# Value products of five halves in eight on high and low parts, placed behind the projection's heads, in a cross-attention and gated feed-forward kernel

## The reference

```python
x  = layer_norm(features);  lat = layer_norm(latents)         # features: ctx, latents: x
q  = lat @ Wq;  kv_in = concat([x, lat], axis=1)              # 128 keys for each sequence
k  = kv_in @ Wk;  v = kv_in @ Wv
sim = einsum('bhqd,bhfd->bhqf', q * scale, k)                 # masked keys: -inf
alphas = softmax(sim)
out = einsum('bhqf,bhfv->bhqv', alphas, v)
x  = x + out.reshape(B, Q, H * DH) @ Wo
# then x + shared(layer_norm(x)) + routed(layer_norm(x)): a gated feed-forward, 8 experts, the best 2 of each token
```

## Time and profile before

| what | us |
| --- | --- |
| median of 3 runs (1104.0 to 1105.6) | 1104.18 |
| the profiled execution | 1103.4 |
| its span, first to last instruction | 1101.7 |
| busy: TensorE 1068.2, DVE 923.9, ScalarE 793.7, GpSimd 615.4 | |
| mean granted clock of TensorE, share of full speed | 0.995 |

### The profile page before, as it was taken

The page is one execution under the profiler, slowest core; times in us unless marked ns, Lnnn a source line. Parts: engine busy times, 40 slices in busy tenths (PEclk is TensorE's granted clock), DMA queues, the critical chain, the costliest instruction groups (busy, mean ns, idle before and its releaser), DMA issues.

```text
span 1101.7 us, 28185 instructions
## 1 busy us (share of the span) xinstructions
PE 1068.2 (97%) x7732; PEld 930.6 (84%) x7732; DVE 923.9 (84%) x4092; ACT 793.7 (72%) x2927; POOL 615.4 (56%) x717
## 2 busy tenths in 40 slices
PE   5799999999999999999999999999999999999986
PEld 5688888888888888888888888888888888888865
DVE  3778888889888889888888988888988888988866
ACT  3787777777777777777777777777777777777751
POOL 4555565656555656565566555555656565665431
PEclk9999999999999999999999999999999999999999
DMA  5365555555555555555555555555555555555531
GB/s 155 118 179 157 170 163 164 164 162 174 162 166 167 170 162 164 171 162 168 168 166 163 167 168 169 166 165 157 176 166 162 170 164 164 169 159 158 164 90 35
DMA packets 246557, 175.23 MB, mean 159 GB/s; under 512 B 29184, under 2 KB 213632, under 8 KB 246400
## 3 DMA queue, kind: packets, MB, share of 16 engines
q1 hardware_dynamic: 242336, 172.14, 51.6%
q10 hardware_dynamic: 4064, 1.30, 0.5%
HBM read 102.57 MB, written 70.77 MB: 157 GB/s over the span
## 4 chain that ended last, share of the span: by engine, by line
PE 91%; DVE 3%; DMA 2%; SPq 1%; issue 1%; ACT 1%; POOL 0%; ACTq 0%; DVEq 0%; POOLq 0%
PE bank L915 20%; PE bank L892 19%; PE bank L849 15%; PE bank L851 14%; PE bank L850 14%; PE bank L855 6%; PE bank L978 1%; PE bank L930 1%; DMA kv_raw<-in_x 1%; DMA pT<-probsT_dram 1%; SPq L351 1%; PE bank L923 1%; PE bank L967 1%; DVE MV_lo L815 0%; ACT probs L582 0%
## 5 line engine op out<-in xcount | busy, mean ns | idle before, releaser
L470 POOL TENSOR_TENSOR probs<-probs,rdenom 128x512 f32<-128x512 f32 x256 | 266.7, 1042 | 357.4 <-DVE rdenom L713 352.8
L582 ACT ACTIVATE probs<-logits,neg_max 128x128 f32<-128x128 f32 x1024 | 398.9, 396 | 0.9 <-DVE neg_max L704 0.9
L915 PEld LDWEIGHTS bank<-kvT,tT 128*128 128x128 f32 x2048 | 268.8, 192 | 120.8 <-issue 103.7
L915 PE MATMUL bank<-kvT,tT 128*128 128x128 f32 x2048 | 270.6, 275 | 0.0
L892 PE MATMUL bank<-pT,kv_f 128*128 128x512 f32 x512 | 262.7, 595 | 4.5 <-DMA pT<-probsT_dram 4.4
L704 DVE CUSTOM_DVE_ANT_0 logits<-bank,mask_add 128x128 f32<-128x128 f32 x1024 | 232.6, 283 | 6.1 <-PE bank L915 5.9
L749 DVE TENSOR_TENSOR cT_lo<-bank,cT_hi 128x512 fp32r<-128x512 f32 x256 | 175.1, 684 | 57.6 <-ACT cT_hi L544 57.6
L582 ACT ACTIVATION_READ_ACCUMULATOR probs<-logits,neg_max 128x1 f32 x1024 | 197.3, 193 | 0.0
L529 ACT ACTIVATE h_tanh<-bank 128x256 f32<-128x256 f32 x160 | 61.6, 385 | 178.7 <-PE bank L851 172.7
L544 ACT CAST cT_hi<-bank 128x512 fp32r<-128x512 f32 x256 | 150.1, 586 | 44.2 <-PE bank L892 44.1
L719 DVE STREAM_TRANSPOSE probsT<-probs 128x512 f32<-128x512 f32 x253 | 173.9, 687 | 0.5 <-issue 0.5
(11 more groups left out here) (105 smaller groups left out, 1981.1 us busy)
## 6 DMA issues: line engine op xcount, KB each, us to landing
probsT_dram<-probsT SPq DMA_DIRECT2D x253, 256.0 KB, 2.1
pT<-probsT_dram SPq DMA_DIRECT2D x1012, 64.0 KB, 2.1
gates<-gates_dram SPq DMA_DIRECT2D x62, 256.0 KB, 4.1
kv_raw<-in_ctx SPq DMA_DIRECT2D x32, 128.0 KB, 2.8
kv_raw<-in_x SPq DMA_DIRECT2D x32, 128.0 KB, 2.9
mask_raw<-in_mask_BxS_ik SPq DMA_DIRECT2D x32, 128.0 KB, 3.4
x_res<-in_x SPq DMA_DIRECT2D x32, 128.0 KB, 3.2
out<-out_sb SPq DMA_DIRECT2D x32, 128.0 KB, 2.0
```

What stands on the lines that cost most here:

```text
L470: nc.gpsimd.tensor_tensor(by_pair, by_pair, rdenom[n][:, :].unsqueeze(2).unsqueeze(3).broadcast_to([P, PAIRS, P // QUAD, QUAD]), ALU.mult) ...
L582: nc.scalar.activation(probs[c % 4][:, :, r, :] if c < BY_DMA else key_order(c)[:, r, :].rearrange("p (c k) -> p c k", k=QUAD), logits[c % ...
L915: last = nc.tensor.matmul(S_ps[c % 2][:, P * r:P * (r + 1)], tT[:, kl % 4, hd:hd + 2, :], kvT[g % 2][:, kl % 4, :], start=True, stop=True)
```

## The change

For the halves 0, 1, 2, 4 and 6 of each group but the last (155 products of 256) the value product is no longer one `f32` matmul. ScalarE makes a high part `pT_hi` of the probabilities, GpSimd the low part `pT_lo`; once per group they make `kv_hi` and `kv_lo` of the keys. TensorE then does three `f32r` matmuls of 512 columns. They stand in the slot behind the query chunk, the projection's heads and, in slot 6, the transposes of `attnT`, and ahead of the feed-forward tile. Halves 3, 5 and 7 keep their `f32` product at the head of the slot.

The copies of such a product out of PSUM (`cT_hi` on ScalarE, `cT_lo` on DVE) move to the slot after (`products_to_copy`). So slots 1, 3, 5, 6 and 7 copy two, two, one, one and two products, and slots 0, 2 and 4 none. `cT_hi` and `cT_lo` are now single; a semaphore `W_front_done` says that the projection's first eight heads have read the part that halves 0 to 3 fill.

```diff
--- before.py
+++ after.py
@@ -61,6 +61,8 @@
         kv_r = sb("kv_r", [P, GB])
         kv_n = sb("kv_n", [P, GB, D])
         kv_f = [sb(f"kv_f{n}", [P, GB, D]) for n in range(3)]
+        kv_hi = [sb(f"kv_hi{n}", [P, GB, D], f32r) for n in range(3)]
+        kv_lo = [sb(f"kv_lo{n}", [P, GB, D], f32r) for n in range(3)]
         kvT = [sb(f"kvT{n}", [P, GB, P]) for n in range(2)]
         latT_hi = [sb(f"latT_hi{n}", [P, GB, S], f32r) for n in range(2)]
         latT_lo = [sb(f"latT_lo{n}", [P, GB, S], f32r) for n in range(2)]
@@ -76,6 +78,8 @@
         probsT = [sb(f"probsT{n}", [P, PAIRS * P]) for n in range(2)]
         probsT_dram = [nc.dram_tensor(f"probsT_dram{n}", [P, PAIRS * P], fp32, kind="Internal").ap() for n in range(3)]
         pT = [sb(f"pT{n}", [P, PAIRS * P]) for n in range(3)]
+        pT_hi = [sb(f"pT_hi{n}", [P, PAIRS * P], f32r) for n in range(2)]
+        pT_lo = [sb(f"pT_lo{n}", [P, PAIRS * P], f32r) for n in range(2)]
         attnT = sb("attnT", [P, GT])
         x_res = [sb(f"x_res{n}", [P, TT, D]) for n in range(2)]
@@ -105,7 +109,6 @@
         gates_dram = nc.dram_tensor("gates_dram", [E, GT], fp32, kind="Internal").ap()
         h_tanh = sb("h_tanh", [P, GT])
         h_silu = sb("h_silu", [P, GT])
-        h = [sb(f"h{n}", [P, NT + 1, GT]) for n in range(2)]
         out_sb = [sb(f"out_sb{n}", [P, TT, D]) for n in range(2)]
@@ -118,10 +121,11 @@
             wv_raw = su("wv_raw", [P, INNER])
             wo_raw = su("wo_raw", [P, H // 2, D])
             wT = [su(f"wT{n}", [P, H // 2, D]) for n in range(3)]
-            su("unused", [P, 5 * H * DH])
+            su("unused", [P, H * DH])
             w13_stage = [su(f"w13_stage{n}", [P, (NT + 1) * P]) for n in range(2)]
-        cT_hi = [sb(f"cT_hi{n}", [P, GB, 2, PAIRS * P], f32r) for n in range(2)]
-        cT_lo = [sb(f"cT_lo{n}", [P, GB, 2, PAIRS * P], f32r) for n in range(2)]
+        cT_hi = sb("cT_hi", [P, GB, 2, PAIRS * P], f32r)
+        cT_lo = sb("cT_lo", [P, GB, 2, PAIRS * P], f32r)
+        h = [sb(f"h{n}", [P, NT + 1, GT]) for n in range(2)]
         banks = [es.enter_context(nc.psum_tensor(f"bank{n}", [P, 512], fp32)) for n in range(8)]
@@ -168,9 +172,14 @@
         last_pT_in_psum = sem("last_pT_in_psum")
         last_pT_ready = sem("last_pT_ready")
         pT_loaded = [sem(f"pT_loaded{n}") for n in range(3)]
+        kv_hi_ready = sem("kv_hi_ready")
+        kv_lo_ready = sem("kv_lo_ready")
+        pT_hi_ready = sem("pT_hi_ready")
+        pT_lo_ready = sem("pT_lo_ready")
         C_in_psum = sem("C_in_psum")
         cT_hi_ready = sem("cT_hi_ready")
         cT_lo_ready = sem("cT_lo_ready")
+        W_front_done = sem("W_front_done")
         W_in_psum = sem("W_in_psum")
         attnT_ready = sem("attnT_ready")
         attn_in_psum = sem("attn_in_psum")
@@ -197,6 +206,7 @@
         GATE_STEPS = 12
         KV_STEPS = 6
+        SPLIT_HALVES = (0,1,2,4,6)
         X2_STEPS = 4
         PROJ_HEADS = (0, 2, 4, 6, 8, 12, 16)
         HT = NT + 1
@@ -251,6 +261,20 @@
             if k == 0:
                 return (6, 0) if has(j, p, 0, NG - 1) else None
             return query_chunk(j, p, k - 1)
+
+        def split_before(c):
+
+
+            return len(SPLIT_HALVES) * (c // HALVES) + sum(k < c % HALVES for k in SPLIT_HALVES)
+
+        def has_split(c):
+
+            return 0 <= c < HALVES * (NG - 1) and c % HALVES in SPLIT_HALVES
+
+        def products_to_copy(e):
+
+
+            return [c for c in (e - 5, e - 4) if has_half(c) and has_split(c) == (c == e - 5)]
         def head_columns(cT, hd):
@@ -461,6 +485,17 @@
                 i = 2 * j + p
                 for k in range(HALVES):
                     e = HALVES * i + k
+                    if has_split(e - 4):
+                        c = e - 4
+                        n = split_before(c)
+                        pool.wait_ge(pT_hi_ready, n + 1)
+                        nc.gpsimd.tensor_tensor(pT_lo[n % 2][:, :], pT[c % 3][:, :], pT_hi[n % 2][:, :].bitcast(fp32),
+                                                ALU.subtract).then_inc(pT_lo_ready, 1)
+                    if k == 1 and has(j, p, -1, NG - 2):
+                        g = i + 1
+                        pool.wait_ge(kv_hi_ready, g + 1)
+                        nc.gpsimd.tensor_tensor(kv_lo[g % 3][:, :, :], kv_f[g % 3][:, :, :], kv_hi[g % 3][:, :, :].bitcast(fp32),
+                                                ALU.subtract).then_inc(kv_lo_ready, 1)
                     if has_half(e):
                         n = e % 4
@@ -510,6 +545,16 @@
                 nc.scalar.mul(MV_hi[q // 4][:, bank_heads(q % 4), :], banks[q][:, :].rearrange("p (h d) -> p h d", h=4),
                               -SCALE if q < 4 else 1.0).then_inc(MV_hi_ready, 1)
+            def high_part(c):
+                g, kl = c // HALVES, c % HALVES
+                act.wait_ge(C_in_psum, c + 1)
+                if kl == 0:
+                    after(act, W_front_done, g)
+                if kl == 4:
+                    after(act, W_in_psum, g)
+                nc.scalar.copy(by_quad(cT_hi[:, kl % 4, kl // 4, :]),
+                               C_ps[c % 2][:, :].rearrange("p (a r q) -> p a r q", r=PAIRS, q=QUAD)).then_inc(cT_hi_ready, 1)
+
             def project(i):
                 act.wait_ge(W_in_psum, i)
                 after(act, attn_in_psum, i - 1)
@@ -521,6 +566,14 @@
                     e = HALVES * i + k
                     if k == attn_half(i) and i == NG:
                         project(i)
+                    if has_split(e - 4):
+                        c = e - 4
+                        n = split_before(c)
+                        act.wait_ge(pT_loaded[c % 3], 64 * (c // 3 + 1))
+                        after(act, C_in_psum, c - 1)
+                        nc.scalar.copy(pT_hi[n % 2][:, :], pT[c % 3][:, :]).then_inc(pT_hi_ready, 1)
+                    if e - 5 in products_to_copy(e):
+                        high_part(e - 5)
                     tile = ffn_tile(j, p, k - 1) if k else None
                     if tile is not None:
                         n = tile[1]
@@ -535,14 +588,8 @@
                         after(act, S_in_psum, HALVES * (i + ahead - 1) + (4 if c < 4 else 8))
                         nc.scalar.copy(tT[:, :, 2 * c:2 * c + 2, :].rearrange("p b h q -> p h b q"),
                                        query_bank(c, e - 1)[:, :].rearrange("p (h b q) -> p h b q", h=2, b=GB)).then_inc(t_ready, 1)
-                    if has_half(e - 4):
-                        c = e - 4
-                        g, kl = c // HALVES, c % HALVES
-                        act.wait_ge(C_in_psum, c + 1)
-                        if kl == 0:
-                            after(act, W_in_psum, g - 1)
-                        nc.scalar.copy(by_quad(cT_hi[g % 2][:, kl % 4, kl // 4, :]),
-                                       C_ps[c % 2][:, :].rearrange("p (a r q) -> p a r q", r=PAIRS, q=QUAD)).then_inc(cT_hi_ready, 1)
+                    if e - 4 in products_to_copy(e):
+                        high_part(e - 4)
                     if i == NG and k < 3:
                         c = BY_DMA + k
                         act.wait_ge(last_pT_in_psum, k + 1)
@@ -584,6 +631,11 @@
                                                  logits[c % 2][:, r, :].rearrange("p (c k) -> p c k", k=QUAD),
                                                  ACT.Exp, bias=neg_max[c % 2][:, r:r + 1], scale=-1.0,
                                                  accum_out=denom[c % 4][:, r:r + 1]).then_inc(exp_done, 1)
+                    if k == 0 and has(j, p, -1, NG - 2):
+                        g = i + 1
+                        act.wait_ge(kv_step, KV_STEPS * (g + 1))
+                        after(act, C_in_psum, HALVES * (g - 2))
+                        nc.scalar.copy(kv_hi[g % 3][:, :, :], kv_f[g % 3][:, :, :]).then_inc(kv_hi_ready, 1)
                     if k == 6 and has(j, p, 2, NG - 1):
                         act.wait_ge(gate_step, GATE_STEPS * (i - 1))
                         after(act, gates_loaded, 32 * (i - 2))
@@ -740,15 +792,16 @@
                         gate_part(*{3: (3, 4), 4: (9,)}[k])
                     if k in (3, 4) and i < LAST:
                         gate_part({3: 5, 4: 10}[k])
-                    if has_half(e - 4):
-                        c = e - 4
+                    for c in products_to_copy(e):
                         g, kl = c // HALVES, c % HALVES
                         dve.wait_ge(cT_hi_ready, c + 1)
                         if kl == 0:
-                            after(dve, W_in_psum, g - 1)
-                        nc.vector.tensor_tensor(by_quad(cT_lo[g % 2][:, kl % 4, kl // 4, :]),
+                            after(dve, W_front_done, g)
+                        if kl == 4:
+                            after(dve, W_in_psum, g)
+                        nc.vector.tensor_tensor(by_quad(cT_lo[:, kl % 4, kl // 4, :]),
```

(19 more changed lines are left out.)

## The result

| | before | after |
| --- | --- | --- |
| median, us | 1104.89 (4 runs, 1104.0 to 1106.27) | 1172.83 (4 runs, 1170.83 to 1173.83) |
| ratio to before, 95% interval | | 1.0619 (1.0602 to 1.0635) |
| the profiled execution, us | 1103.4 | 1173.77 |
| its span, us | 1101.7 | 1172.0 |

The forecast was 1157, the upper end of the range 1170. The direction was right, and the time lies 3 us above the range.

What follows compares the result with a forecast made beforehand. TensorE was taken to bound the kernel, with DVE deciding in slots 2 to 4. 29 x 1.30 = 37.7, plus 17.1 for slot 0, less 1.4, gave 53 us on 1103.4: 1157 us, range 1105 to 1170.

Steps and rivals of the forecast that it cites:

- The product itself: Each split product on TensorE: 0.70 us instead of 0.86, scaled by columns, saving 0.16 us each.
- The bank wait of 0.31: Slots 2, 4, 5, 6: query chunk waits 0.31 us for ScalarE's copy; slots 5 and 6 0.15 us longer each.
- Slot 0, 0.57: Slot 0: 0.50 us wait for the copy, 0.23 for `pT_lo`, less 0.16 saved; 0.57 us longer.
- Slots 2 to 4, "I take 1.0": Slots 2 to 4: DVE's `g_ahead` meets GpSimd's `pT_lo`, delaying `h` and slot 4's tile; 1.0 us longer, bounds 0 and 1.27.
- Edits costed at nothing: `kv_hi`, `kv_lo`, single `cT`, SyncE's queue, clock: 0 us; without idle cover in slot 0, `x2` transposes late, 0.3 us a frame.
- The sum, 29 x 1.30 + 30 x 0.57 - 1.4: Slots 2 to 6 in 29 frames, slot 0 in 30, less nine early products' savings: 53 us together.
- The range: Whole kernel: 1105 to 1170 us, leaving out no more than the faster case and the upper part of "more is late".
- more is late: Rival, chance 0.10: GpSimd's added operations delay scaling and transposes in slots 0 to 2, another 0.5 us a frame; 1172 us.
- GpSimd and DVE didn't miss each other: Rival, chance 0.24: the two miss each other, so slots 2 to 4 grow only about 0.1 us; 1131 us.
- The bank wasn't free in time: Rival, chance 0.11: chunk's copy ends by T + 0.75 in slots 2, 5, 6, so TensorE never waits; 1079 us.
- the faster case: Rival, chance 0.11: bank free in time, all 155 products save 0.16 us each; 1079 us.
- The gauge of 0.8 us of new waits in a frame: Test for the faster case: if a frame's new waits sum to under 0.8 us, the kernel is faster.

Runs made afterwards that it cites:

- the fastest version: Changed kernel with only halves 1 and 2 split, query-chunk copy first, `kv_hi` in slot 4, `kv_lo` a frame later, GpSimd's slot-3 `h` products in slot 4: 1085.99 us.
- the kernel with the spare instruction: Kernel before plus one unused 512-element GpSimd instruction per frame ahead of `kv_ve` in slot 3: 1129.52 us, ratio 1.0223.

## Why the prediction was right in direction and 16 us too low

The step that failed is the size of two terms and what was put at nothing for the two ends of the run. Slots 2 to 4 were taken as 1.0 us longer and became 1.24, slot 0 as 0.57 and became 0.72; that is 0.39 us in each frame, 10 us of the 17 that the profiled executions differ from the sum. The other 7 us lie before frame 4 and behind frame 30. The mechanisms themselves, the uncovered copy and the gate held by GpSimd, were the right ones.

- **The product itself** (0.86 to 0.70): right to the hundredth, scaled by columns. The figure of the Trainium skill (TensorE: Matmul & The Clock Gate, section Back-to-back issue gap) of 131 ns for 512 columns in a stream doesn't hold for this `f32r` stream, which took 0.23 to 0.24 us each, beside 0.12 for 256 columns.
- **The bank wait of 0.31** in slots 2, 4, 5 and 6: measured 0.30. Slots 5 and 6 became 0.16 longer each, against 0.15. Shown by the kernel with the move alone (+30 us) and by the copy first (-20 us).
- **Slot 0, 0.57:** too small by 0.15. The wait for the copy and the place behind `x_r` came as worked out; `pT_lo` ended 3.47 us into the slot, where 577.89 less 574.45 made 3.44. What the term lacked is the product behind a wait: 0.81 us, not the 0.70 of a stream, since its first matmul holds TensorE 0.34 us. The rest is some hundredths in each step.
- **Slots 2 to 4, "I take 1.0":** 1.24. The mechanism was right, with its place and its partner: `g_ahead` met `pT_lo` and ended 0.16 after it, and half 0 alone gives back 30 us. From the end of the `h` products everything came as worked out, `g_ahead` 1.62 us behind it. What was off is how early DVE gets there. The term treated the `cT_lo` that leaves slot 2 and the one added in slot 3 as equal. In the trace DVE comes to `g_one` 0.87 us earlier than before (2.61 instead of 3.48 us behind the start of slot 2), `g_one` is held by the first `h` product and gives 0.57 of it back, and the second `cT_lo` takes 0.60. So DVE starts `g_ahead` 0.29 us later than before, and 0.29 and the 0.95 of `g_ahead` make the 1.24. The prediction had looked only at instructions with two tensors in SBUF; `g_one` has one. But the 0.24 isn't the price of `g_one` alone: with the copy first it runs free, and slots 2 to 4 are no shorter, since `g_gt` is held longer in its place.
- **"Edits costed at nothing", `kv_hi`:** the cover named for it, idle time on ScalarE at the end of slot 0, is not there. In the kernel after, slot 1 is no longer than before (4.62), since slot 0 is long enough; as soon as slot 0 is short, the cast costs 0.43 us a frame, 12 us in all. The text priced its loss at 0.3 us and on the wrong reader (the transposes of `x2`, not the chunk). It didn't harm the forecast, but it hid why a smaller form of the change doesn't pay.
- **The sum, 29 x 1.30 + 30 x 0.57 - 1.4:** the frame grew by 2.26 us, not by 1.87. Between the starts of frames 4 and 30 that makes 10 of the 17 us missed. At the start of frame 4 (the start of its slot 0) the changed kernel is 6.3 us late, where the sum has 2 x 1.87 - 1.4 = 2.3. From frame 30 to the end it loses 5.4 more, where the sum has 2.5. What these 4 and 3 us are made of was not tested. A part may be the clock, which the prediction put at nothing: it is lower at the start, as said above, and the changed kernel is 0.8 us late at its first scores, where no product has been made yet.
- **The range:** it ended at 1170 and so took in only part of the case "more is late" (1172). Another 0.39 us a frame is near the 0.5 of that case, but not by its mechanism: slot 1, which holds the transposes of `x2`, is no longer than before. That 1172 comes so close to the measured 1172.83 is luck.
- **The rivals.** GpSimd and DVE didn't miss each other (32 waits for `h`, once a frame). The bank wasn't free in time. The copy put first shows what the faster case had left out: with no wait for the bank in slots 2 to 6 the kernel still takes 1152.85 us. The gauge of 0.8 us of new waits in a frame stands for five split halves; no kernel with five came under it, and the fastest version, with two, has none.
- **Contention:** the Trainium skill (GPSIMD Engine Reference, section Specifications) names the contention between GpSimd and DVE instructions with two SBUF inputs or in a two-port mode. The first half is what `g_ahead`, `g_tie`, `g_eq` and `g_dense` show. `g_one` (one tensor, SBUF to SBUF) would be the second half, though no run isolates a mode. That it doesn't hold beside every GpSimd instruction is shown by `g_ahead` at 0.28 us beside `kv_r` (four elements), before and in the kernel with the spare instruction.

The 68 us in the runs' own terms: the place of the products alone costs 30, and taking half 0 out of the kernel after gives back 30. The two are read in different kernels and don't add exactly, since the waits of slots 2 and 4 lie beneath the gate's; what is left lies in slot 0 and at the two ends.

## What to carry to other kernels

Before moving an instruction that is dear, ask what it hides: here 0.86 us of product in front of a single-buffered bank covered another engine's tanh and copy, and the move alone cost more than the cheaper product could ever save. Work given to an idle GpSimd isn't free because it is idle: look which DVE instructions run beside it, since some are held until it ends, and put it beside those that nobody waits for. A copy that moves to a later slot keeps its bank that much longer: ask which product needs this bank next. And cost a once-a-group cast by who stands behind it in its queue, not by the engine's idle time.

## What the runs showed of the hardware

- A stream of `f32r` matmuls with 512 columns starts one every 0.23 to 0.24 us, twice the 0.12 of 256 columns. Behind a wait for data the first one takes 0.34 us until the next starts.
- Some DVE instructions beside a GpSimd one over 512 elements (or 256) took up to a microsecond more than alone: `g_ahead` 0.28 and 1.23, `g_tie` 0.32 and 1.26, `g_dense` 0.17 and 1.15, `g_one` 0.15 and 0.71. Where both ends were looked at, it ended 0.03 to 0.16 us after the GpSimd instruction. It hardly depends on its own size: `g_dense` and `g_one` have 16 elements in a partition.
- Not every one is held. Beside the same kind of GpSimd instruction `h`, which reads a bank of PSUM, kept its 0.42 us, `cT_lo`, which does too, its 0.69, and `kv_bn` its 0.28. With five and with four halves and the copy first, `g_one` started 0.01 us ahead of the `h` product and took 0.14.
- ScalarE and GpSimd weren't held in this way in the frame looked at: its five casts `pT_hi` took 0.60 to 0.61 us, its five `pT_lo` 1.28 to 1.30 us.
